# One-hots of the last layer's sums: made on GpSimd, one tile behind each gather, instead of on VectorE

## What is computed

```python
res = project(mobius_add(hyper_tail, hyper_rel))
res = jax.nn.relu(logmap(res, hyper_head) + ricci * 1e-07)
sums = zeros((n_entities, 64)).at[head].add(res)
```

## Time and profile before

| | us |
|---|---|
| median of 3 runs | 5221.54 (5216.28 to 5222.11) |
| span of the profiled execution | 6351.7 |
| its last layer's two edge loops, first gather to last product of sums | 3205.9 to about 6323 |
| busy in the span: VectorE / GpSimd / TensorE / ScalarE | 3726.5 / 3463.1 / 2842.1 / 1728.7 |

### The profile page before, as it was taken

The page is one execution under the profiler, slowest core; times in us unless marked ns, Lnnn a source line. Parts: engine busy times, 40 slices in busy tenths (PEclk is TensorE's granted clock), DMA queues, the critical chain, the costliest instruction groups (busy, mean ns, idle before and its releaser), DMA issues. The chain is left out here.

```text
span 6351.7 us, 75027 instructions
## 1 busy us (share of the span) xinstructions
PE 2842.1 (45%) x17919; PEld 2271.2 (36%) x17920; DVE 3726.5 (59%) x6870; ACT 1728.7 (27%) x5084; POOL 3463.1 (55%) x3375
## 2 busy tenths in 40 slices
PE   4544588433343334477614434434431343444442
PEld 1333456223333333345403333333331233333332
DVE  6444544255555666444426776667673767667678
ACT  0255200011111111000003354344340335445434
POOL 5667445466555663544265565566525556556551
PEclk7655699666666666678855555555555555555555
DMA  3720400355555554400021111111102111111110
GB/s 101 171 94 1 127 1 1 105 154 172 167 171 169 173 173 143 139 4 1 8 49 42 37 42 37 37 41 38 33 10 50 40 37 42 37 39 41 41 30 13
DMA packets 470914, 446.71 MB, mean 70 GB/s; under 512 B 113322, under 2 KB 417773, under 8 KB 470268
## 3 DMA queue, kind: packets, MB, share of 16 engines
q1 hardware_dynamic: 230602, 227.94, 12.4%
q0 software_dynamic: 116768, 136.51, 9.0%
q10 hardware_dynamic: 123282, 79.08, 4.5%
HBM read 306.93 MB, written 136.34 MB: 70 GB/s over the span
## 5 line engine op out<-in xcount | busy, mean ns | idle before, releaser
L2412 POOL DMA_INDIRECT tg<-tab_d,tail_ids x1632 | 1711.2, 1049 | 1191.1 <-DVEq L2731 644.9
L458 POOL DMA_INDIRECT sorted_edges_d<-place_batch x784 | 825.0, 1052 | 657.1 <-issue 220.6
L2437 PE MATMUL hr<-near_table,near_hot 128*128 x4896 | 654.4, 278 | 926.2 <-issue 593.1
L1598 POOL DMA_INDIRECT xg<-tab_d,src_i x784 | 768.0, 980 | 501.1 <-issue 241.6
L2445 PE MATMUL acc<-msg,sum_hot 128*96 128x65 f32 x3264 | 559.8, 364 | 902.1 <-ACT msg L2519 701.3
L2437 PEld LDWEIGHTS hr<-near_table,near_hot 128*128 128x128 f16 x4896 | 505.6, 108 | 1075.7 <-issue 970.2
L2445 PEld LDWEIGHTS acc<-msg,sum_hot 128*96 128x96 f32 x3264 | 536.4, 277 | 924.8 <-issue 924.7
L2492 ACT ACTIVATE pr<-hr 128x396 f32<-128x396 f32 x576 | 272.2, 482 | 1235.0 <-DMA b2col<-in_L_gnn_be_dram 786.9
L2513 ACT ACTIVATE pr<-pr,coef_c 128x64 f32<-128x64 f32 x1496 | 380.7, 340 | 82.4 <-issue 79.4
L2506 ACT ACTIVATE msg<-tg,coef_b 128x64 f32<-128x64 f32 x1632 | 399.1, 340 | 2.6 <-DVEq L2926 2.6
L2743 DVE TENSOR_REDUCE scal<-prod 128x17 f32<-128x1088 f32 x288 | 370.5, 1286 | 9.8
(11 more groups left out here) (504 smaller groups left out, 5392.9 us busy)
## 6 DMA issues: line engine op xcount, KB each, us to landing
ex<-spread_d SPq DMA_DIRECT2D x112, 448.0 KB
msg_d<-back ACTq DMA_DIRECT2D x112, 448.0 KB
near_hot<-head_row_d SPq DMA_DIRECT2D x96, 408.0 KB
tg<-tab_d,tail_ids POOLq DMA_INDIRECT x1632
spread_d<-zeros ACTq DMA_DIRECT2D x28, 896.0 KB
spread_d<-zeros SPq DMA_DIRECT2D x28, 896.0 KB
idsU<-dst_short_d SPq DMA_DIRECT2D x112, 224.0 KB
pairs_d<-pair_m SPq DMA_DIRECT2D x3, 4800.0 KB
```

Of the source, the lines that this page charges most:

```text
L458: l.eng.indirect_dma_start(K.sorted_edges[:, :], bass.IndirectOffsetOnAxis(ap=K.batch[:, n % 2, 0, k:k + 1], axis=0), K.batch[:, n % 2, 1, ...
L1598: l.eng.indirect_dma_start(xg[j.c % ROWS][:, half * H + k, :], None, K.tab1, bass.IndirectOffsetOnAxis(ap=src_i[:, t:t + 1], axis=0)).then ...
L2412: e.indirect_dma_start(tg[:, u % TAILS * GQ + k, :], None, K.tab3, bass.IndirectOffsetOnAxis(ap=K.tail_ids[:, u * GQ + k:u * GQ + k + 1], ...
L2437: ins = e.matmul(hr[(u * FILLS + g) % 2][:, c:c + PW3], near_hot[u % HOTS][:, k, :], rows[:, bass.ds(at[k] + n * PW3, PW3)], start=n == 0, ...
```

## The change

The one-hots `sum_hot` are no longer made by VectorE in `gather_up`. GpSimd makes them, one tile (128x96, `tensor_scalar` with `is_equal`, the head's number as the scalar of each partition) behind each gather from quarter 6 on: behind gather k of quarter u comes tile k of the one-hots of quarter u - 6. They have three buffers in place of two; before the first tile of quarter v GpSimd waits for `added` of quarter v - 3. Five quarters of one-hots come behind the last gather, the last quarter's behind the four relation products of L2418. The node numbers are read from SBUF (`nodes`), the copy to PSUM goes. The ring of tails has eight quarters in place of nine, which pays for the third buffer. A scratch row `yy` moves from SBUF to PSUM.

```diff
-TAILS = 9
+TAILS = 8
+SUMS = 3
+SUM_LAG = 6
-    sum_hot = two("sum_hot", [P, GQ, BN], F32)
+    sum_hot = [sb(f"sum_hot{r}", [P, GQ, BN], F32) for r in range(SUMS)]
-    sc = sb("scal", [P, 30, M], F32)
+    sc = sb("scal", [P, 29, M], F32)
-    names, kA = near_dve[:, 0:BN], [near_dve[:, BN + s * M:BN + (s + 1) * M] for s in range(2)]
+    gap, kA = near_dve[:, 0:M], [near_dve[:, (s + 1) * M:(s + 2) * M] for s in range(2)]
         e.wait_ge(tails_stored, 16)
+        e.wait_ge(shaped, 2 - hop)
+        def sum_tile(v, k):
+            if k == 0 and v >= SUMS:
+                e.wait_ge(added, v - SUMS + 1)
+            ins = e.tensor_scalar(sum_hot[v % SUMS][:, k, :], nodes[:, :], K.head_keys[:, v * GQ + k:v * GQ + k + 1], None, ALU.is_equal)
+            if k == GQ - 1:
+                ins.then_inc(sum_made, 1)
         (gather of tile k of quarter u, as before)
+                if u >= SUM_LAG:
+                    sum_tile(u - SUM_LAG, k)
+        for v in range(QUARTERS - SUM_LAG, QUARTERS - QN + SUMS):
+            for k in range(GQ):
+                sum_tile(v, k)
         e.wait_ge(coefs, MSTEPS)
         (the four relation products, as before)
+        for v in range(QUARTERS - QN + SUMS, QUARTERS):
+            for k in range(GQ):
+                sum_tile(v, k)
 gather_up(u):
-            if u >= 2:
-                v.wait_ge(added, u - 1)
-            v.tensor_tensor(sum_hot[u % 2][:, :, :], K.head_keys[...].to_broadcast([P, GQ, BN]),
-                            names.unsqueeze(1).to_broadcast([P, GQ, BN]), ALU.is_equal).then_inc(sum_made, 1)
-        v.wait_ge(shaped, 1)
-        v.tensor_copy(names, nodes[:, :]).then_inc(l.sem, l.add(1))
-            yy = A1(29)
+            yy = gap
```

More of the change, by code:

```diff
@@ L2444, in add @@
             for k in range(GQ):
-                ins = e.matmul(sums[:, bass.ds(at[k], D + 1)], sum_hot[u % 2][:, k, :], msg[u % QN][:, k, :], start=False, stop=False, skip_group_check=True)
+                ins = e.matmul(sums[:, bass.ds(at[k], D + 1)], sum_hot[u % SUMS][:, k, :], msg[u % QN][:, k, :], start=False, stop=False, skip_group_check=True)
             ins.then_inc(added, 1)
@@ L2572, in gather_up @@
             s, t = turn(u)
-            if u >= 2:
-                v.wait_ge(added, u - 1)
-            v.tensor_tensor(sum_hot[u % 2][:, :, :], K.head_keys[:, u * GQ:(u + 1) * GQ].unsqueeze(2).to_broadcast([P, GQ, BN]),
-                            names.unsqueeze(1).to_broadcast([P, GQ, BN]), ALU.is_equal).then_inc(sum_made, 1)
             p_, r_, out = pr[s][:, t, 0:D], pr[s][:, t, RW:RW + D], msg[u % QN][:, :, 0:D]
```

## The result

The changed kernel takes **6244.9 us** (median of 4 runs, 6240.29 to 6249.95) beside 5221.8 us (4 runs, 5216.28 to 5228.43) of the kernel before: ratio 1.196, interval 1.1946 to 1.1974, **1023 us slower**. The forecast was 5580 us, with 5760 as its upper end. The direction was right and the size was not.

What follows compares the result with a forecast made beforehand. GpSimd and VectorE were taken as level at 92 to 94 us a step. Per hop 714 tiles by 0.30 us, +214, less 29 and 5, gave +180; two hops +360, 5221.5 to 5580 us, range 5130 to 5760.

Steps and rivals of the forecast that it cites:

- the price of the tile itself: One GpSimd one-hot tile between gathers: 0.22 us for itself, of 0.30 us a tile in all.
- the port's term: GpSimd's tile meeting VectorE instructions with two SBUF inputs at SBUF's ports: 0.08 us a tile.
- the slack: At a hop's end GpSimd may lag 29 us before VectorE starves; taken off the 214 us a hop.
- The 5 us for the tail: Behind a hop's last coefficients four VectorE one-hot instructions (7.4 us) go: 5 us a hop saved.
- The stalls are the profiler's gift: Last layer's edge loops: VectorE's three stalls, 31.1 us a step, and GpSimd's 645 us idle are not in the runs.
- Part 1: One-hots taken from VectorE: 7.4 us a step, 178 us in all; none booked inside the loop, GpSimd being level.
- Rings of tails: Eight rings in place of nine: no cost; were ScalarE later than the marks, up to 6 us a step.
- The wait for `added`: GpSimd's new wait, with gathers queued behind it: no cost, as TensorE is half a step ahead in every quarter.
- (a): Rival: the tile hides in the 0.30 us gap before a gather; 5120 or about 5210 us; chance 0.08 with gain, 0.03 without.
- (b): Rival: VectorE's stalls are real in the runs too, leaving GpSimd 27 us idle a step; 5130 us; chance 0.1.
- (c): Rival: a GpSimd tile costs 0.5 us, 323 us a hop; 5870 us; chance 0.08.
- (d): Rival: tiles hold VectorE at the ports, 7 us a step, giving back its saving; 5220 us, no change; chance 0.03.

## Why the prediction was wrong

**The size of the loss, from the runs.** Per hop, gather 102 to the last: 4410.45 - 2946.73 = 1463.7 us against 3905.39 - 2950.53 = 954.9 us, so +508.8 us; from the last gather to the last coefficients +2.7 us (46.5 against 43.9). The second hop's gathers give +504.4 us in the same way and its end +2.4. That is 1018 of the 1023 us; the rest lies outside the gathers' rhythm. Of the 0.71 us by which the mean pair grew (2.05 against 1.34), 0.52 stand where nothing disturbs it (1.77 against 1.25), of which the instruction of eight columns is 0.29 and 88 columns are 0.23; the other 0.19 come from the meetings with VectorE, since 23% of the tiles between gathers take over 0.7 us, 1.38 at the mean against 0.55: 0.23 by 0.83 is 0.19.

- **Step that failed: the price of the tile itself**, 0.22 us taken, 0.52 us measured. The row nearest in engine and input count misled me: two affine selects 0.25 us apart. The two-input row, 0.38 us each, was nearer and served only for the upper end, which at 0.5 us a tile was still short. That upper end held nothing for the port. The choice that the prediction made, a tile hidden in the gap or a tile paid in full, was also no either-or: behind every added instruction the gap shrinks, from 0.30 us to between 0.16 and 0.25. But the gather beside a tile is 0.07 to 0.09 us longer and the tile starts 0.04 us behind it, so of a tile of 0.55 us 0.52 are paid.
- **Also failed: the port's term**, 0.08 us taken, 0.19 measured. I treated meeting a product with two SBUF inputs as chance. It is not: the rows above show the pairs locked to VectorE's rhythm of 2.72 us, and 124 of 128 dot products meet a tile. Each pair that needs 1.77 us waits there for the next product's end. The Trainium skill has the rule (SBUF — State Buffer, section Who interferes with whom): a VectorE instruction with two SBUF inputs contends with a GpSimd instruction that reads SBUF, not with one that only writes it. Both halves agree with this case: of 330 tiles that start within such an instruction 312 take over 0.7 us, while none of 447 fills does. The 72 tiles that start beside the products with A, whose other operand lies in PSUM, are not held either.
- **Also failed: the slack**, 29 us taken, 2 us measured. It was read from a profile of the other level, in which GpSimd had been ahead. The 5 us for the tail were not there either: behind the last gather VectorE's same instructions take 42.7 us in place of 39.2 beside GpSimd's 85 tiles, 0.35 us of it in the dot products and the rest in the long chain of small ones. With the sum's own form, 714 by 0.71 is 507 us a hop; less 29 and 5 it would have been 473, so slack and tail are worth 77 us of the miss of 663, and the price 585 (2 by 714 by 0.41).
- **"The stalls are the profiler's gift": wrong reason, right use.** The stalls belong to a level that whole sessions have, profiled or not. The count that was to confirm it was wrong in part: ScalarE's idle time before `back` in layer 2 is 446.7 us at the lower level too (829.8 at the upper), so the 448.9 us can't be added whole; of the 1126 us between the two profiles 396 lie ahead of the last layer's first gather, and 730 behind it, where the three stalls make 535. The stalls were not in the runs to be forecast, and taking them out was right; the level of GpSimd and VectorE (92 and 93.8 us forecast, 91.0 and 91.1 measured) stood on it, and so did the sign. But the forecast for the profiled span, -50 to +80 us, has no meaning, since the two profiles stand at different levels.
- **Part 1 was right**: of VectorE's 7.4 us a step 14 us in all come back. That the third quarter's C * relation would come late by up to 3.7 us is there as well, 44 times.
- **Rings of tails: right**, free at both levels. **The wait for `added`: right** in price (19.5 us of idle time on GpSimd, two times), but it was not said that TensorE would wait for tiles with the fillings of hr queued behind. That cost nothing visible further, as GpSimd, which hardly waits, sets the step.
- **Rivals.** (a) holds for a write of 0.11 us and for two thirds of one of 0.19 (0.06 us of it are paid); of a tile that reads, 0.52 of 0.55 us are paid. (b) fell for the runs counted. (c), the dearer tile, was the right one at too small a size; its chance of 0.08 was too low, given that no row priced the operation. The range was also said to take in (a), whose 5120 us lie below its lower end of 5130. (d) is there mostly in the opposite direction: VectorE holds GpSimd. Tiles hold VectorE too, 3.5 us behind the first hop's last gather.
- **What the profile should have shown.** Waits for marks under 200 us: yes, 3. VectorE waiting for gathers: yes, 395 us. Gaps between gathers of 0.5 us or more: more, 0.76 undisturbed and 1.71 beside the products. Tiles of 0.2 us: no, 0.55 to 1.5.

**Open.** What sets the two levels (by the recorded numbers not the chip, since one gave both), and why an edit that takes work away is slower at the upper one. The changed kernel was seen only beside the lower level, so its ratio at the upper is unknown.

## What to carry to other kernels

Work given to GpSimd between gathers is priced per instruction: moving one wide VectorE instruction (1.85 us) into 17 narrow ones there cost 12 us, where one wide instruction took 2.9 (a subtract of the same shape; a compare in that form was not run). Before a bound is read from a profile, its span is set against the runs, and if they differ by a fifth, every slack and wait in it is of another execution. Where no row shows the operation, the upper bound must hold the dearest row's price and the port's wait together.

## What the runs showed of the hardware

- Behind a gather, a one-input GpSimd instruction of 128 partitions adds 0.29 us at 8 columns (compare) and 0.52 us at 96, there whatever the operation (compare, add) and whether the scalar is a constant or a column; a fill of 96 columns, 0.19 us long, adds 0.06 us. The Trainium skill (GPSIMD Engine Reference, section Engine selection) calls one-input elementwise work on GpSimd roughly line-rate. The tiles here don't agree: 2.6 ns a column and 0.3 us fixed, where VectorE's 1632 columns in 1.85 us are 1.1 ns a column.
- 0.30 us lie ahead of each gather. A write of 0.11 us behind the gather before leaves the gathers 1.25 us apart, as without it; a fill of 0.19 us leaves 1.31 us in place of 1.25.
- The stream of gathers and tiles on GpSimd locks to VectorE's dot products with two SBUF inputs: 2.72 us a pair in place of 1.77. A fill, which reads nothing, isn't held by them (0.30 us at most in 447), but it is by VectorE's one-input f16 compare of 2176 columns (0.68 us, 22 of 22).
- The kernel before has two levels, 5222 and 6300 us, by session; at the upper, ScalarE issues one instruction every 0.7 to 1.4 us in stretches, waiting for nobody that the profile shows.
